# Both layer norms of attention applied by ScalarE, one power and an offset by GpSimd for two tiles, and another order of VectorE in the last pair

## What is computed

```python
def layernorm(x): return (x - mean(x)) / sqrt(var(x) + 1e-5)        # over the 256 columns
q = (layernorm(x) @ Wq.T + bq) ; k, v = context @ Wk.T + bk, context @ Wv.T + bv
attn = softmax(q @ k.T / 4) ; out = (attn @ v) @ Wo.T + bo           # head by head
x = x + tanh(g_xattn) * out
xf = layernorm(x)
x = x + tanh(g_ffn) * (experts(xf) + shared(xf))   # 16 experts, the two best of each token by xf @ Wg
```

## Time and profile before

| | us |
|---|---|
| median of 3 runs | 578.85 |
| lowest, highest | 578.63, 579.65 |
| the profiled execution, its own time | 582.2 |
| its span, from the first to the last instruction | 580.4 |

### The profile page before, as it was taken

One profiled execution on the slowest core, in us unless ns is written; L12 is line 12 of the kernel. 1 busy time (PEld: TensorE's weight loads), 2 busy tenths in 40 slices (PEclk: granted clock), 3 DMA queues, 4 the chain that ended last, 5 costly groups with the idle time before them and its releaser, 6 DMA issues.

```text
span 580.4 us, 11843 instructions
## 1 busy us (share of the span) xinstructions
PE 551.8 (95%) x3230; PEld 443.7 (76%) x3231; DVE 361.2 (62%) x846; ACT 227.6 (39%) x763; POOL 327.3 (56%) x261
## 2 busy tenths in 40 slices
PE   8878989989987999988999999999999999999997
PEld 6545765665756888867888888888888888888886
DVE  7558778778766872224656665556665556535687
ACT  0787878878886311111222222122222122233232
POOL 5477788888876255671445755474464470226660
PEclk9899999999998999999999999999999999999999
DMA  8671010000020225244266877557557210013442
GB/s 279 270 277 41 24 29 19 28 27 18 28 82 20 92 86 213 89 139 152 102 209 213 281 278 259 188 187 290 185 189 284 87 54 29 28 47 90 119 119 90
DMA packets 32897, 76.07 MB, mean 131 GB/s; under 512 B 4960, under 2 KB 21856, under 8 KB 29920
## 3 DMA queue, kind: packets, MB, share of 16 engines
q1 hardware_dynamic: 14960, 52.44, 25.2%
q10 hardware_dynamic: 14832, 14.82, 8.0%
q0 software_dynamic: 3072, 8.39, 4.7%
HBM read 54.93 MB, written 18.61 MB: 127 GB/s over the span
## 4 chain that ended last, share of the span: by engine, by line
PE 74%; POOL 6%; issue 5%; DVE 5%; DMA 5%; ACT 3%; SPq 1%; DVEq 0%; POOLq 0%; ACTq 0%
PE mid L701 14%; PE big L682 7%; PE big L683 7%; PE big L684 7%; POOL sorted_x L1537 5%; PE work L442 4%; PE big L473 4%; PE mid L486 4%; PE mid L692 4%; PE big L603 3%; PE big L604 3%; PE big L605 3%; PE work L505 3%; DMA sorted_x<-xf_all,pos 2%; PE last L498 2%
## 5 line engine op out<-in xcount | busy, mean ns | idle before, releaser
L868 ACT ACTIVATE last<-arena 128x512 f32<-128x512 f32 x47 | 28.3, 602 | 183.3 <-DVE arena L1319 183.3
L792 ACT ACTIVATE arena<-big,nmax 128x128 f32<-128x128 f32 x256 | 90.3, 395 | 4.7 <-DVE nmax L984 4.5
L701 PE MATMUL mid<-dring,arena 128*128 x376 | 88.9, 379 | 0.0
L1319 DVE TENSOR_TENSOR arena<-big,bring 128x512 f32<-128x512 f32 x47 | 32.5, 692 | 88.2 <-PE big L684 88.2
L682 PE MATMUL big<-u_hi,xsT_hi 128*128 x188 | 81.8, 435 | 0.9 <-issue 0.9
L1445 POOL TENSOR_TENSOR arena<-arena,rinv 128x1024 f32<-128x1024 f32 (+1 forms) x32 | 59.7, 1865 | 32.7 <-DVE rinv L992 32.7
L1469 POOL TENSOR_TENSOR u_lo<-arena,u_hi 128x2048 fp32r<-128x2048 f32 x16 | 74.4, 4648 | 1.3
L701 PEld LDWEIGHTS mid<-dring,arena 128*128 128x128 f32 x376 | 67.8, 190 | 7.4
L684 PE MATMUL big<-u_hi,xsT_lo 128*128 x188 | 73.5, 391 | 0.0
L683 PE MATMUL big<-u_lo,xsT_hi 128*128 x188 | 73.4, 390 | 0.0
L792 ACT ACTIVATION_READ_ACCUMULATOR arena<-big,nmax 128x1 f32 x256 | 60.2, 235 | 0.0
(11 more groups left out here) (168 smaller groups left out, 1159.4 us busy)
## 6 DMA issues: line engine op xcount, KB each, us to landing
arena<-up_w_dram SPq DMA_DIRECT2D x16, 1024.0 KB, 7.6
bring<-expert_bias_dram SPq DMA_DIRECT2D x16, 640.0 KB, 5.3
dring<-down_w_dram SPq DMA_DIRECT2D x18, 512.0 KB, 3.3
sorted_y<-arena ACTq DMA_DIRECT2D x47, 128.0 KB, 1.8
arena<-sorted_x ACTq DMA_DIRECT2D x43, 128.0 KB, 2.2
sorted_x<-dring SPq DMA_DIRECT2D x3, 1536.0 KB, 8.6
arena<-ctx_t_dram ACTq DMA_DIRECT2D x8, 256.0 KB, 2.7
dring<-up_w_dram SPq DMA_DIRECT2D x2, 1024.0 KB, 4.8
```

Source lines behind the costliest of these rows:

```text
L701: i = mm(mid[:, 1, 0:D], gT[:, p, c, :], dring[:, slot, c * D:(c + 1) * D], start=(c == 0), stop=(c == HC - 1))
L792: i = nc.scalar.activation(probs[:, u % 2, h, :], big[:, u % 2, h // 4, (h % 4) * CTX:(h % 4 + 1) * CTX], ACT.Exp, bias=nmax[:, u % 2, h:h ...
```

## The change

The parts of the norms are dealt out anew; what is computed stays.

VectorE's `norm_var` also makes the negated mean (`nm1`, `nm2`), and where the norm is applied by ScalarE, its own `ln1_apply` and `ln2_apply` are gone: ln1 of pairs 2 to 7, ln2 of pairs 0 to 5. Pairs 0 and 1 of ln1 and 6 and 7 of ln2 stay as they were. GpSimd makes the power for two tiles at once in both norms, in unit 1, and behind each power an offset, negated mean times power (`off1`, `off2`), which waits for the power by a semaphore of its own (`ln1_pow`, `ln2_pow`). ScalarE applies both norms in unit 1 behind the copy of the heads, `norm_xf` for pair j-1 and `norm_xn` for pair j+2: Identity with the power as scale and the offset as bias. In the last pair VectorE's instructions stand in another order. Declarations of tiles and semaphores are left out here.

```diff
@@ -812,11 +818,27 @@
                 act.wait_ge(xfT_ready, j + 1)
                 nc.scalar.activation(xfT_hi[:, :, bass.ds(2 * P * j, 2 * P)], xfT[:, :, :], ACT.Copy).then_inc(xfT_hi_kept, 1)
 
+            def norm_xf(j):
+                act.wait_ge(ln2_rstd, 2 * j + 2)
+                if not (isinstance(j, int) and j < 1):
+                    act.wait_ge(xf_kept, 32 * j)
+                    act.wait_ge(xfT_ps, j)
+                for b in range(2):
+                    nc.scalar.activation(xfs[:, b, :], x_all[:, 2 * j + b, :], ACT.Identity, bias=off2[:, b:b + 1],
+                                         scale=rs2[:, b:b + 1]).then_inc(xf_ready, 1)
+
+            def norm_xn(j):
+                act.wait_ge(ln1_rstd, 2 * j + 2)
+                act.wait_ge(xnT_ps, j)
+                for b in range(2):
+                    nc.scalar.activation(xn[:, b, :], x_all[:, 2 * j + b, :], ACT.Identity, bias=off1[:, b:b + 1],
+                                         scale=rs1[:, b:b + 1]).then_inc(xn_ready, 1)
+
             def load_context(j):
                 act.wait_ge(v_ps, j)
                 act.dma_start(ctxT, ctx_t[j]).then_inc(ctx_loaded, 16)
 
-            def pair(j, ahead, ahead2, behind2):
+            def pair(j, ahead, ahead2, behind, behind2):
                 for u in range(UNITS):
                     copy_probs(j, u)
                     if behind2 and u == 0:
@@ -826,18 +848,22 @@
                     elif ahead:
                         exps(j + 1, u - 2)
                     copy_heads(j, u)
+                    if behind and u == 1:
+                        norm_xf(j - 1)
+                    if ahead2 and u == 1:
+                        norm_xn(j + 2)
                     if u == 2 and ahead2:
                         load_context(j + 2)
 
             act.wait_ge(bias_loaded, 16)
             exps(0, 0)
             exps(0, 1)
-            pair(0, True, True, False)
-            pair(1, True, True, False)
+            pair(0, True, True, False, False)
+            pair(1, True, True, True, False)
             with act.Fori(2, LAST - 1) as j:
-                pair(j, True, True, True)
-            pair(LAST - 1, True, False, True)
-            pair(LAST, False, False, True)
+                pair(j, True, True, True, True)
+            pair(LAST - 1, True, False, True, True)
+            pair(LAST, False, False, False, True)
 
             act.wait_ge(raw_odd, 16)
             for n in range(NEXT_PIECES):
@@ -941,15 +967,19 @@
 
                 v.memset(carrier[:, :], 0.0)
 
-            def norm_var(src, mv, ve, b, done):
+            def norm_var(src, mv, ve, nm, b, done):
                 carry()
                 link(v.bn_stats(stats[:, b, :], src))
                 carry()
                 link(v.bn_aggr(mv[:, b, :], stats[:, b, :]))
+                if nm is not None:
+                    v.tensor_scalar(nm[:, b:b + 1], mv[:, b, 0:1], -1.0, None, ALU.mult)
                 v.tensor_scalar(ve[:, b:b + 1], mv[:, b, 1:2], EPS, None, ALU.add).then_inc(done, 1)
 
             def ln1_stats(j, b):
-                norm_var(x_all[:, 2 * j + b, :], mv1, ve1, b, ln1_var)
+                if not (isinstance(j, int) and j < 1):
+                    dve.wait_ge(ln1_rstd, 2 * j)
+                norm_var(x_all[:, 2 * j + b, :], mv1, ve1, None if isinstance(j, int) and j < 2 else nm1, b, ln1_var)
 
             def ln1_apply(j, b):
                 dve.wait_ge(ln1_rstd, 2 * j + b + 1)
@@ -968,7 +998,9 @@
             def ln2_stats(j, b):
                 n = 2 * j + b
                 dve.wait_ge(o_taken, n + 1)
-                norm_var(x_all[:, n, :], mv2, ve2, b, ln2_var)
+                if not (isinstance(j, int) and j < 1):
+                    dve.wait_ge(ln2_rstd, 2 * j)
+                norm_var(x_all[:, n, :], mv2, ve2, None if isinstance(j, int) and j >= LAST - 1 else nm2, b, ln2_var)
 
             def ln2_apply(j, b):
                 n = 2 * j + b
@@ -1086,28 +1118,28 @@
 
             def last_slot(u):
                 j = LAST
-                if u < 2:
-                    add_attention(j - 1, u)
                 if u == 0:
+                    add_attention(j - 1, 0)
                     row_max(j, 2)
                     row_inv(j, 1)
                     normalise_upper(j, 1)
                     ln2_stats(j - 1, 0)
                     row_max(j, 3)
+                if u == 1:
+                    add_attention(j - 1, 1)
                     row_inv(j, 2)
+                    copy_upper(j, 1)
                     normalise_upper(j, 2)
-                    copy_upper(j, 1)
+                    ln2_stats(j - 1, 1)
                     ln2_apply(j - 1, 0)
-                elif u > 1:
-                    copy_upper(j, u)
-                if u == 1:
-                    ln2_stats(j - 1, 1)
                     ln2_apply(j - 1, 1)
+                    row_inv(j, 3)
                 if u == 2:
-                    row_inv(j, 3)
+                    copy_upper(j, 2)
                     normalise_upper(j, 3)
                     copy_xfT(j - 1)
                 if u == 3:
+                    copy_upper(j, 3)
                     choose_copy(j - 1)
                     choose(j - 1)
 
@@ -1140,16 +1172,10 @@
                         (copy_k, copy_q)[u](j + 1)
                     if ahead2 and u == 1:
                         ln1_stats(j + 2, 1)
-                    if behind and u < 2:
-                        ln2_apply(j - 1, u)
-                    if ahead2 and u == 1:
-                        ln1_apply(j + 2, 0)
                     if ahead and behind and u == 2:
                         copy_v(j + 1, 1 - slot)
                     if behind and u == 2:
                         copy_xfT(j - 1)
-                    if ahead2 and u == 2:
-                        ln1_apply(j + 2, 1)
                     if behind and u == 3:
                         choose_copy(j - 1)
                         choose(j - 1)
@@ -1407,17 +1433,30 @@
             g = nc.gpsimd
 
             def rstd1(j, tiles=slice(0, 2)):
+                early = isinstance(j, int) and j < 2
                 pool.wait_ge(ln1_var, 2 * j + tiles.stop)
                 if not (isinstance(j, int) and j < 1):
                     pool.wait_ge(xn_ready, 2 * j)
                 n = tiles.stop - tiles.start
-                g.tensor_tensor(rs1[:, tiles], ve1[:, tiles], mhalf[:, :].to_broadcast([P, n]), ALU.pow).then_inc(ln1_rstd, n)
-
-            def rstd2(j, b):
-                pool.wait_ge(ln2_var, 2 * j + b + 1)
+                i = g.tensor_tensor(rs1[:, tiles], ve1[:, tiles], mhalf[:, :].to_broadcast([P, n]), ALU.pow)
+                if not early:
+                    i.then_inc(ln1_pow, 1)
+                    pool.wait_ge(ln1_pow, j - 1)
+                    i = g.tensor_tensor(off1[:, :], nm1[:, :], rs1[:, :], ALU.mult)
+                i.then_inc(ln1_rstd, n)
+
+            def rstd2(j, tiles=slice(0, 2)):
+                late = isinstance(j, int) and j >= LAST - 1
+                pool.wait_ge(ln2_var, 2 * j + tiles.stop)
                 if not (isinstance(j, int) and j < 1):
                     pool.wait_ge(xf_ready, 2 * j)
-                g.tensor_tensor(rs2[:, b:b + 1], ve2[:, b:b + 1], mhalf[:, :], ALU.pow).then_inc(ln2_rstd, 1)
+                n = tiles.stop - tiles.start
+                i = g.tensor_tensor(rs2[:, tiles], ve2[:, tiles], mhalf[:, :].to_broadcast([P, n]), ALU.pow)
+                if not late:
+                    i.then_inc(ln2_pow, 1)
+                    pool.wait_ge(ln2_pow, j + 1)
+                    i = g.tensor_tensor(off2[:, :], nm2[:, :], rs2[:, :], ALU.mult)
+                i.then_inc(ln2_rstd, n)
 
             def spread_keys(j, u):
 
@@ -1486,8 +1525,10 @@
                         normalise(j, u + 1)
                     elif ahead:
                         normalise(j + 1, 0)
-                    if behind and u < 2:
-                        rstd2(j - 1, u)
+                    if isinstance(j, int) and j == LAST and u < 2:
+                        rstd2(j - 1, slice(u, u + 1))
+                    elif behind and u == 1:
+                        rstd2(j - 1)
                     if behind2 and u == 0:
                         keep_xfT(j - 2)
                         keep_choice(j - 2)
@@ -1525,7 +1566,7 @@
             keep_xfT(LAST - 1)
 
             for b in range(2):
-                rstd2(LAST, b)
+                rstd2(LAST, slice(b, b + 1))
             pool.wait_ge(onehots_ready, 1)
             keep_xfT(LAST)
 
```

More of the change, by code:

```diff
@@ L206, in flamingo_layer @@
         rs2 = sb("rs2", [P, 2])
+        nm1 = sb("nm1", [P, 2])
+        nm2 = sb("nm2", [P, 2])
+        off1 = sb("off1", [P, 2])
+        off2 = sb("off2", [P, 2])
         mhalf = sb("mhalf", [P, 1])
@@ L262, in flamingo_layer @@
         ln1_var = sem("ln1_var")
+        ln1_pow = sem("ln1_pow")
+        ln2_pow = sem("ln2_pow")
         ln1_rstd = sem("ln1_rstd")
```

## The result

| | before | changed |
|---|---|---|
| median, us | 578.78 (578.63 to 579.65, 4 runs) | 573.03 (571.96 to 574.14, 4 runs) |
| ratio | | 0.9883, 95% interval 0.9863 to 0.9903 |
| the profiled execution | 582.2, span 580.4 | 573.39, span 571.6 |

The account below looks back on a forecast made before the run. TensorE, busy 95% of the span, bounds the kernel, so gains come only where it waits. Steady pairs 5.5, pair 0 0, pair 7 1.2: 6.7 us off the 578.85 median gives 572.1, range 569.2 to 576.

Parts of the forecast that it names:

- GpSimd's chain: Steady pairs, worked in pair 3: probabilities, powers, multiplies; offsets of xf at 95.73 and xn at 96.79.
- ScalarE: Steady pairs: four norms at 0.48 us each fit the 1.81 us gap; copies of unit 2 start 0.14 later.
- the sum: Whole kernel: 5.5 us from five steady pairs, 0 from pair 0, 1.2 from pair 7, together 6.7 us.
- Rival C: Steady pairs: ScalarE late, norms costing 0.75 us or address work showing; 0.6 a pair, 3.0 in all, 575.1; 15%.
- The steady pairs: Pairs 1 to 5: TensorE's waits for the copy of v and xn shrink; 1.1 us each, 5.5 together (3.0 to 7.2).
- Pair 0: First pair: copies 1.5 us late, but exps freed from VectorE's row maximum; effects cancel, 0 (-0.5 to +0.3).
- Pair 7: Last pair: VectorE's new order brings the reciprocal of unit 3 and TensorE's last transposes earlier; 1.2 us (0.5 to 1.3).
- A: Case: clock falls in pair 7, 572.1, 52%. As a time (152.2): first weighing to last output projection's start, 162.7 before.
- B: Pair 7: granted clock stays up, giving back about 1.9 us more, until 187; 570.2; 22%.
- The way to the end: After pair 7, routing, scatter and experts: nothing hangs on a fixed time, so the shift is handed on whole.
- rival E: Scatter: its writes share queues with weight loads, taking back some 4 us of the gain; 576.1; 6%.

Follow-up runs that it names:

- the experiment with the dearer norms: Changed kernel with one more 32-column ScalarE instruction, into an unread tile, ahead of each norm: 582.18 us, ratio 1.0014 to the kernel before.
- the two orders alone: Kernel before with ln1's first half behind the copy of v and VectorE's new order in pair 7: 573.25 us (0.9876), then 570.41 (0.9845).
- the one move alone: Kernel before, VectorE keeping both norms, with ln1's first half written behind the copy of v: 577.15 us, ratio 0.9844.

## Why the prediction was right, point by point

**GpSimd's chain: right.** Forecast were the offsets of xf and xn 12.5 and 13.6 us into pair 3; they came at 12.5 and 13.5 (93.47 and 94.50 from 81.00). The two-column multiply took 0.19, as bounded from below.

**ScalarE: right.** Two norms took 1.09 alone and 0.99 to the next, so about 0.50 each against the 0.48 of the sum, and 0.59 for a single one as worked out (the row in the experiment with the dearer norms). The copies started 14.7 us into the pair, against 14.6 forecast and 14.5 before. The gap took the norms and had nothing left. Rival C was a real danger, but its price was too low: norms at 0.75 instead of 0.48 are 1.1 us more on ScalarE in a pair, and it put 0.6 a pair on that. In the experiment 1.2 us more cost 1.2 a pair, by which C would be some 5 us (an estimate) and not 3.0.

**The steady pairs: right in mechanism, a little low in size.** 1.1 us a pair were taken and pair 3 gained just that, from 21.76 to 20.66; but pair 3 was one of the shortest of the five, and the mean gain is 1.3: 6.5 us, not 5.5.

**Pair 0: the step that failed.** The sum had two effects cancelling to 0, with a low end of -0.5. ScalarE's copies did come late, by 1.4 us counted from the first weighing, and the exps behind were on time, 9.3 us behind the first weighing as before (33.56):

```profile
31.61 1.09 ACT L834 ACTIVATE arena<-x_all,off,rs 128x256 f32<-128x256 f32 x2 [0.81 <-POOL off L1445]
32.60 1.06 ACT L808 ACTIVATE arena<-mid 128x512 f32<-128x512 f32 x2
```

but nothing in the sum asked what the wait in between does to TensorE: 2.30 us idle, after which the granted clock fell in two of the four profiles with this code, for 1.6 us. With the clock up, 0 is right (14.15 and 14.16 against 14.13). The forecast weighed the clock in pair 7 and not here.

**Pair 7: the order right, the likeliest case wrong.** Forecast were 1.2 us, with the clock falling as before (A), and 1.9 more if it stayed (B). B came: 2.4 in all, 0.9 of it from the waits up to the last transposes and 1.5 of the 1.9 from the clock (4.08 us from there to the end of the pair, now 2.58). The forecast's ground for B was thin: it set busy for half against 57%, but by its own rows TensorE was busy for 2.87 of the 5 us ahead of the last transposes, and is for 2.99 of them now. The 0.9 is less than 1.2, although GpSimd's last probabilities start 1.0 earlier and end 1.5 earlier. VectorE's and GpSimd's rows show why. VectorE's multiply of the upper heads, before and now:

```profile
181.20 0.69 DVE L996 TENSOR_TENSOR arena<-arena,rinv 128x512 f32<-128x512 f32 x1
```

```profile
173.85 0.41 DVE L1010 TENSOR_SCALAR xfs<-x_all,mv,rs 128x256 f32<-128x256 f32 x1 [0.45 <-POOL rs L1454]
174.18 0.20 DVE L1024 RECIPROCAL rinv<-rsum 128x8 f32<-128x8 f32 x1
...
174.85 1.19 DVE L1028 TENSOR_TENSOR arena<-arena,rinv 128x512 f32<-128x512 f32 x1
```

GpSimd's multiplies of units 2 and 3 now:

```profile
170.72 1.04 POOL L1484 TENSOR_TENSOR arena<-arena,rinv 128x512 f32<-128x512 f32 x1 [0.42 <-DVE rinv L1024]
...
174.46 1.04 POOL L1484 TENSOR_TENSOR arena<-arena,rinv 128x512 f32<-128x512 f32 x1 [0.64 <-DVE rinv L1024]
```

GpSimd's 512 columns take 1.04 us instead of 1.54, and VectorE's multiply of the upper heads 1.19 instead of 0.69: of the two that meet, the one that starts first goes through and the second is held by half a microsecond. Before, VectorE started at 181.20 and GpSimd at 181.25; now GpSimd starts at 174.46 and VectorE at 174.85. TensorE's last transposes come 0.11 us after VectorE's multiply ends (176.04) and 0.65 after GpSimd's (175.50), so by the times they wait for VectorE now, though the profile names no releaser:

```profile
176.15 1.06 PE L492 MATMUL mid<-const,arena 128*128 128x128 f32 x8 [0.42 <-issue]
```

(The Trainium skill, "SBUF — State Buffer", Who interferes with whom, has a VectorE instruction with two inputs in SBUF and a GpSimd instruction that reads SBUF exclude one another, whichever starts first; these rows agree in which of the two is held, and it lost 0.50 us, somewhat less than the 0.64 and 0.65 that the other had left. The forecast applied the Trainium skill's rule to the norms only, and these took 0.41 us each.)

**The way to the end: right.** From the last output projection to the first scatter it is 18.0 us in all the profiles, and the scatter with GpSimd's cast behind it takes 52.0 to 52.5. The first expert matmuls follow 3.2 to 8.4 us later, for the most part by how fast the scattered rows come back: the longest (4.9 to 8.4) were all in one comparison, whose kernel before took 586.5. That is where the profiles differ most from one comparison to the next. Whether it also blurred the 3 us between the two orders alone and the changed kernel in their first comparison stays open: in the profiled executions of those two, what follows attention is equally long within 0.1. Nor did rival E come: behind attention the profile gained 0.6, and its premise, queues shared with the loads of weights, isn't what the profile's page shows: q0, the only software queue, has 8.39 MB, which is just the 64 indirect transfers of 128 KB, and the plain ones are on q1 and q10.

**The sum.** In the profiled executions the gain was 8.8: 6.5 in the steady pairs, 2.4 in pair 7, 0.7 lost up to pair 1 (1.6 lost, 0.9 won by an earlier first weighing), 0.6 behind attention. The 0.9 isn't the change's: the first weighing is at 25.20 in the kernel before, but at 24.36 and 24.30 in the two kernels that only reorder VectorE later on, and at 24.27, 24.58 and 25.01 in the changed one. What the trace shows of the change is 6.5+2.4-1.6 = 7.3, and where the clock stays up in pair 0, 8.9. The forecast's 6.7 was 1.0 too low in the steady pairs and 1.2 in pair 7 and left out 1.6 in pair 0: that the sum came so close is luck, because errors in both directions met. The medians differ by 5.75, less than any of these sums, and why isn't shown. The profiled execution of before was 3.4 above its median, and its trace is the only one of that comparison; what the other executions did can't be told. By comparisons, 0.9883, 0.9880 and 0.9901 agree.

What came is A with B's clock and a loss in pair 0. That the work had to leave VectorE was never tested by the forecast, and it was wrong to leave out the simplest alternative: the gain of the steady pairs comes from writing one instruction further down. With the order of pair 7 beside it A is 152.2, the shortest of all that were run. The ratios don't rank so finely: 0.9845 and 0.9876 for this kernel, 0.9844 for the one move alone, though its A is 2.5 longer.

## What to carry to other kernels

When an engine's queue is held by an instruction that waits, look first whether that instruction can stand later in the same queue; moving it to another engine fills a gap there that something else may need, and costs preparation (here a negated mean and an offset). An idle time of an engine is free only where it would wait anyway: in the steady pairs the norms of xn cost nothing in front of ScalarE's copies and 0.7 us a pair behind them. And for every wait that an edit creates or closes on TensorE, ask also what it does to the clock, at each place where it stands, the first pair as well as the last.

## What the runs showed of the hardware

The granted clock turned a saved 0.9 us into 2.4 in pair 7. After a wait of 2.30 us in pair 0 it fell in two profiles of four, which cost 1.6, and stayed up in the other two. A 512-column multiply of VectorE and one of GpSimd, both on tiles in SBUF, take 0.69 and 1.54 us when VectorE starts first (181.20 before 181.25) and 1.19 and 1.04 us when GpSimd does (174.46 before 174.85). An ACTIVATE of 256 columns with two per-partition operands takes 0.59 us alone and starts 0.49 to 0.50 behind the one ahead of it in a row; a GpSimd power of two columns 0.70, a multiply of two columns 0.19.
